# A software-pipelined graph network kernel: the hand-written order of all four engines' steps is replaced by another order

## The reference

```python
h = max(layernorm(x), 0);  x = x + cheb(h, adj)      # 4 Chebyshev orders of L = I - D^-1/2 A D^-1/2
h = max(layernorm(x), 0);  x = x + att_net(h, adj)   # h1 = tanh(h We + be), two attention layers, 3-layer MLP
#   v, q, k = tanh(h @ w + b);  att = softmax((q k^T) * mask - 9e15 * (1 - mask));  h' = att @ v
#   z = relu([h2, h3] W1 + b1);  z = relu(z W2 + b2);  z W3 + b3
h = max(layernorm(x), 0);  x = x + relu(norm(adj + I) @ (h @ Wg))
h = max(layernorm(x), 0);  t = adj @ h;  x = x + where(t > 0.5, 1, 0 * t)
```

## Time and profile before

| | |
|---|---|
| median of 3 runs | 851.47 us (851.32 to 852.67) |
| the profiled execution's own time | 851.93 us |
| its span in the profile | 849.8 us |
| PE busy | 768.0 us, 90% |
| DVE, ACT, POOL busy | 66%, 52%, 43% |

### The profile page before, as it was taken

One profiled execution on the slowest core, in us unless ns is written; L12 is line 12 of the kernel. 1 busy time (PEld: TensorE's weight loads), 2 busy tenths in 40 slices (PEclk: granted clock), 3 DMA queues, 4 the chain that ended last, 5 costly groups with the idle time before them and its releaser, 6 DMA issues.

```text
span 849.8 us, 11643 instructions
## 1 busy us (share of the span) xinstructions
PE 768.0 (90%) x3846; PEld 538.0 (63%) x3880; DVE 560.4 (66%) x1631; ACT 445.5 (52%) x929; POOL 363.6 (43%) x492
## 2 busy tenths in 40 slices
PE   7787999989999998999999898999989899998865
PEld 4455666766766676766667576676767667665533
DVE  4656677676767767676776768676676867675432
ACT  3164727474563747466473746547374645726330
POOL 4343545253444526354453525345461634542200
PEclk9999999999999999999999999999999999999995
DMA  6000102020010202010020202002020200000000
GB/s 189 28 2 6 51 1 63 1 62 1 13 51 1 62 1 62 0 39 25 1 63 1 62 1 63 1 1 63 1 62 1 63 1 6 2 0 7 1 6 6
DMA packets 29323, 22.77 MB, mean 27 GB/s; under 512 B 19536, under 2 KB 21072, under 8 KB 29264
## 3 DMA queue, kind: packets, MB, share of 16 engines
q1 hardware_dynamic: 28272, 21.80, 8.9%
q10 hardware_dynamic: 992, 0.23, 0.1%
HBM read 19.93 MB, written 2.10 MB: 26 GB/s over the span
## 4 chain that ended last, share of the span: by engine, by line
PE 53%; POOL 15%; issue 15%; DVE 12%; ACT 5%; POOLq 0%; ACTq 0%; DVEq 0%
PE turn_ps L1155 13%; PE pre_ps L1021 8%; PE post_ps L1021 4%; PE pre_ps L1038 4%; POOL rstd_pre L448 3%; PE turn_ps L1138 3%; POOL k_lo L525 2%; PE pre_ps L980 2%; DVE h_nat_pre L760 2%; POOL centred_pre L451 2%; PE qkv_ps L1089 2%; DVE score_ps L853 2%; PE qkv_ps L1094 2%; PE post_ps L1170 2%; DVE h_nat_pre L752 2%
## 5 line engine op out<-in xcount | busy, mean ns | idle before, releaser
L639 ACT ACTIVATE negz<-negz,negmax 128x512 f32<-128x512 f32 x128 | 92.2, 721 | 64.3 <-DVE negmax L861 64.2
L448 POOL TENSOR_TENSOR rstd_post<-vareps_post,nhalf 128x4 f32<-128x4 f32 x32 | 32.8, 1024 | 203.1 <-DVE vareps_post L742 203.1
L1155 PE MATMUL turn_ps<-pt,v_n 128*128 128x512 f32 x256 | 115.2, 592 | 0.0
L853 DVE TENSOR_TENSOR score_ps<-score_ps,a_nat 128x512 f32<-128x512 f32 x128 | 89.1, 696 | 17.6 <-PE score_ps L1124 16.7
L861 DVE CUSTOM_DVE_ANT_0 negz<-score_ps,gate 128x512 f32<-128x512 f32 x128 | 88.6, 692 | 4.4
L598 ACT ACTIVATE y_t_pre<-pre_ps 128x512 f32<-128x512 f32 x48 | 28.7, 597 | 115.0 <-PE pre_ps L1021 115.0
L1021 PE MATMUL pre_ps<-at_hi,u_pair_pre 128*128 128x512 f32 x192 | 84.8, 441 | 2.9 <-DVE u_pair_pre L780 2.6
L646 ACT ACTIVATE pt<-turn_ps 128x512 f32<-128x512 f32 x128 | 74.0, 592 | 17.9 <-PE turn_ps L1138 15.8
L448 POOL TENSOR_TENSOR rstd_pre<-vareps_pre,nhalf 128x4 f32<-128x4 f32 x32 | 33.9, 1060 | 113.5 <-DVE vareps_pre L742 113.5
L1138 PEld LDWEIGHTS turn_ps<-ident,negz 128*128 128x128 f32 x512 | 60.7, 140 | 32.5 <-issue 15.9
L1138 PE MATMUL turn_ps<-ident,negz 128*128 128x128 f32 x512 | 75.4, 275 | 1.9 <-ACT negz L639 1.7
(11 more groups left out here) (157 smaller groups left out, 1764.0 us busy)
## 6 DMA issues: line engine op xcount, KB each, us to landing
a_nat<-in_adj SPq DMA_DIRECT2D x15, 1024.0 KB, 6.1
x_in<-in_x SPq DMA_DIRECT2D x16, 128.0 KB, 2.8
out<-x_out SPq DMA_DIRECT2D x16, 128.0 KB, 1.9
a_nat<-in_adj SPq DMA_DIRECT2D x4, 256.0 KB, 4.8
cheb_ws<-in_L_gnn_weight ACTq DMA_DIRECT2D x2, 64.0 KB, 3.3
att_w<-in_L_gnn_a_wv SPq DMA_DIRECT2D x2, 64.0 KB, 3.8
att_w<-in_L_gnn_a_wk SPq DMA_DIRECT2D x2, 64.0 KB, 3.6
att_w<-in_L_gnn_a_wq SPq DMA_DIRECT2D x2, 64.0 KB, 3.3
```

What stands on the lines that cost most here:

```text
L448: gp.tensor_tensor(rstd[t][:], vareps[t][:], nhalf[:, 0:RB], ALU.pow)\
L639: sc.activation(probs[:, i, :], negz[:, i, :], ACT.Exp, bias=negmax[:, i:i + 1], scale=-1.0, accum_out=total[:, i:i + 1]).then_inc(probs_d ...
L853: ve.tensor_tensor(score_ps[i % 2][:], score_ps[i % 2][:], a_nat[s][:, i, :], ALU.mult)\
L1155: mm = te.matmul(turn_ps[0][:], v_n[a][:, j * P:(j + 1) * P], pt[:, j, :], start=(j == 0), stop=(j == RB - 1))
```

## The change

Only the two tables are rewritten. Every step is still there once for each graph, and no step's code is touched.

```diff
 ORDER = {
     "tensor": """
-        queries.1-1 turn_a0-0 turn2.2-2 turn3.2-2 keys.1-1 turn_a1-0 spread_inv.2-2 values.1-1
-        turn_a2-0 turn_a3-0 attend.2-2 scores0.1-1 cheb_ht-0 scores1.1-1 scores2.1-1 mlp1-2
-        turn0.1-1 cheb_weights-0 scores3.1-1 turn1.1-1 mlp2-2 turn2.1-1 cheb_prop3-0 turn3.1-1
-        mlp3-2 cheb_fold3-0 spread_inv.1-1 attend.1-1 cheb_prop2-0 queries.2-1 cheb_fold2-0
-        gcn_prop-2 keys.2-1 gcn_fold-2 cheb_prop1-0 scores0.2-1 cheb_fold1-0 values.2-1 scores1.2-1
-        scores2.2-1 turn0.2-1 last_prop-2 enc_ht-0 scores3.2-1 turn1.2-1 encode-0 last_fold-2""".split(),
+        queries.1-1 turn_a0-0 turn3.2-2 turn_a1-0 keys.1-1 attend.2-2 turn_a2-0 turn_a3-0
+        scores0.1-1 spread_inv.2-2 scores1.1-1 cheb_ht-0 values.1-1 scores2.1-1 mlp1-2
+        cheb_weights-0 scores3.1-1 turn0.1-1 turn1.1-1 mlp2-2 cheb_prop3-0 turn2.1-1 turn3.1-1
+        mlp3-2 cheb_fold3-0 spread_inv.1-1 attend.1-1 cheb_prop2-0 queries.2-1 gcn_prop-2
+        cheb_fold2-0 keys.2-1 gcn_fold-2 cheb_prop1-0 scores0.2-1 cheb_fold1-0 scores1.2-1
+        values.2-1 scores2.2-1 turn0.2-1 last_prop-2 enc_ht-0 scores3.2-1 last_fold-2 encode-0
+        turn1.2-1 turn2.2-1""".split(),
     "scalar": """
-        exp3.2-2 queries.1-1 copy_pt2.2-2 copy_pt3.2-2 copy_at0-0 keys.1-1 row_sum0-0 copy_at1-0
-        row_sum1-0 values.1-1 copy_at2-0 row_sum2-0 copy_at3-0 copy_inv.2-2 row_sum3-0 cheb_ht-0
-        exp0.1-1 exp1.1-1 copy_pt0.1-1 mlp1-2 exp2.1-1 copy_pt1.1-1 mlp2-2 exp3.1-1 copy_pt2.1-1
-        cheb_copy3-0 copy_pt3.1-1 copy_inv.1-1 cheb_copy2-0 queries.2-1 gcn_copy-2 keys.2-1
-        cheb_copy1-0 values.2-1 exp0.2-1 exp1.2-1 copy_pt0.2-1 enc_ht-0 last_copy-2 exp2.2-1
-        encode-0 copy_pt1.2-1""".split(),
+        values.2-2 copy_pt0.2-2 encode-1 exp3.2-2 copy_pt1.2-2 queries.1-1 copy_pt2.2-2
+        copy_pt3.2-2 copy_at0-0 copy_at1-0 keys.1-1 copy_at2-0 copy_at3-0 copy_inv.2-2
+        row_sum0-0 row_sum1-0 row_sum2-0 cheb_ht-0 row_sum3-0 exp0.1-1 exp1.1-1 values.1-1
+        mlp1-2 exp2.1-1 copy_pt0.1-1 copy_pt1.1-1 exp3.1-1 mlp2-2 cheb_copy3-0 copy_pt2.1-1
+        copy_pt3.1-1 copy_inv.1-1 cheb_copy2-0 queries.2-1 gcn_copy-2 keys.2-1 cheb_copy1-0
+        exp0.2-1 exp1.2-1 last_copy-2 enc_ht-0 exp2.2-1""".split(),
     "vector": """
-        stats_cheb-0  invert.2-2  norm_cheb-0 split_at0-0 split_at1-0
-        split_at2-0 split_at3-0 attend.2-2 mask0.1-1 mask1.1-1 cheb_ht-0 mask2.1-1 
-        cheb_weights-0 mask3.1-1  invert.1-1  mlp3-2
-        cheb_fold3-0 stats_gcn-2 attend.1-1 norm_gcn-2 cheb_fold2-0 gcn_fold-2 stats_last-2
-        mask0.2-1 cheb_fold1-0 stats_enc-0 norm_last-2 mask1.2-1 norm_enc-0 mask2.2-1 enc_ht-0  mask3.2-1  last_fold-2""".split(),
+        stats_cheb-0 invert.2-2 split_at0-0 split_at1-0 norm_cheb-0 split_at2-0 split_at3-0
+        mask0.1-1 attend.2-2 mask1.1-1 cheb_ht-0 mask2.1-1 cheb_weights-0 mask3.1-1 invert.1-1
+        mlp3-2 stats_gcn-2 cheb_fold3-0 attend.1-1 norm_gcn-2 cheb_fold2-0 gcn_fold-2
+        stats_last-2 mask0.2-1 cheb_fold1-0 stats_enc-0 norm_last-2 mask1.2-1 norm_enc-0
+        mask2.2-1 enc_ht-0 mask3.2-1 last_fold-2""".split(),
     "gpsimd": """
-        norm_cheb-0 add_cheb_bias-0 split_qk.1-1 mask_bias-1 roots-0 cheb_u3-0 more_roots-0
-        norm_gcn-2 split_qk.2-1 cheb_f0-0 norm_last-2 norm_enc-0
-        add_mlp_bias-0""".split(),
+        norm_enc-1 norm_cheb-0 mask_bias-1 split_qk.1-1 add_cheb_bias-0 roots-0 cheb_u3-0
+        more_roots-0 norm_gcn-2 split_qk.2-1 cheb_f0-0 add_mlp_bias-1 norm_last-2""".split(),
 }
```

## The result

The changed kernel takes 818.88 us (818.30 to 820.25, 4 runs) against 852.07 before (4 runs): a ratio of 0.9615, 95% interval 0.9602 to 0.9628. The profiled execution took 818.34 us with a span of 816.2.

A forecast was written before the change was run, and what follows sets the result against it. PE was taken as the bound, with about 4.5 of each 49.00 us period waiting. 13 periods at 1.3 (16.9), plus 1.3 and 1.0, minus 0.9, made 18.3: 851.93 to 833.6, stated as 833.5 us, range 823 to 848.

The forecast's parts named there:

- c1's add: DVE's c add ahead of `cheb_prop1`, 1.52 beside POOL's q_lo before, was to run with q_lo already over.
- The walk: Following the new lists from `attend.1` at 450.36 to the next, with durations from the rows: period 47.45 instead of 49.00.
- ACT's part ahead of `queries.1`: `copy_pt0.2` behind `exp2.2` and `values.2` ends near 474.95, ACT's `encode` near 475.6; `queries.1` starts there, 0.2 worse.
- `norm_cheb` in DVE's chain: Between `queries.1` and `scores0.1`: needs the port between q_lo and k_lo, ends near 483.9, then DVE has no gap.
- The rounding up from 47.45 to 47.7: Period taken as 47.7, because every tie (k_lo, `copy_pt0.2`, `norm_cheb`, DVE's chain) can only go one way.
- One reading in the prediction: After `keys.1` in the old trace: `values.1` could start at 479.32, starts at 480.33, 1.0 lost where 0.84 is listed.
- the rounds outside the full ones: Round 2 up to `attend.1` gains 1.3, round 16 about 1.0, the drain loses 0.9.
- More than reckoned: Chance 0.12: the kept stalls at `last_prop` and `keys.1` shrink, period 47.0, 823.5 us.
- The slower rival: Chance 0.13: `mask_bias` ahead of `split_qk.1` on POOL lies fully on the path, its 1.90 added: period 49.6, 860 us.
- Lost ties: Chance 0.22: x3's add waits for POOL's k_lo, or `norm_cheb` for x_b, taking 0.45 to 0.9 a period: 838 to 846 us.
- The signs to look for: Profile after: period near 47.7, `values.1` and `scores2.1` waits gone, `last_prop` 0.8 to 1.1, small ones at `keys.1`, `cheb_weights`.
- The reason that I gave for `last_prop`'s wait: Chain keys.2, k_lo, f0, x1, statistics, `last_prop` is not shortened anywhere; the largest stall of the round stays, 0.25 later.

The follow-up runs named there:

- the first half: Kernel before with the new order only from `queries.1` to `attend.1`, on all engines: 821.61 us, ratio 0.9638, period 47.02.
- the second half: Kernel before with the new order only in the rest of the round and the handover between rounds: 851.60 us, ratio 0.9989, period 48.97.
- the run with the gate back: Changed kernel with POOL's `mask_bias` behind `split_qk.1` again: 819.64 us, ratio 0.9620, period 46.93.
- the last run: Changed kernel with `add_mlp_bias` behind `norm_enc`, plus `keys.2` ahead of `gcn_prop` on PE and of `gcn_copy` on ACT: 836.30 us, ratio 0.9816.
- the run with the row sums back: Changed kernel with ACT's row sums strung between the adjacency copies again, as before the change: 830.40 us, ratio 0.9753, period 47.52.

## Why the prediction was wrong

**The direction and the mechanism were right.** `attend.2` behind `keys.1`, with `values.1` after it, covers the taking of the keys, the adjacency copies and the splits; the first half carries the gain (1.98 of 2.07 in the run of its own), and the second half is even. `last_prop` was to come 19.29 after `attend.1` with its wait left over; it came 451.35 - 432.11 = 19.24 after. c1's add came off q_lo, as stated, and took 0.42. `keys.2`'s place: 9.42 forecast, 9.30 measured.

**The step that failed is the size of a period.** The walk gave 47.45, I wrote 47.7, and it is 46.93. Laid out from `attend.1`, forecast and measured:

| | walk | after |
|---|---|---|
| last_prop | 19.29 | 19.24 |
| queries.1 | 25.25 | 24.99 |
| keys.1 | 27.7 to 27.95 | 27.47 |
| attend.2 | 28.75 | 28.44 |
| scores0.1 | 33.10 | 32.77 |
| mask0.1 on DVE | 34.95 | 34.45 |
| split of h done | 39.20 | 38.54 |
| next attend.1 | 47.45 | 46.93 |

On PE the 0.77 are 0.26 up to `queries.1`, 0.07 from there to `scores0.1`, 0.19 from there to `attend.1`, and 0.25 of rounding up.

- *ACT's part ahead of `queries.1`* was reckoned too long: I let `exp2.2`, `values.2` and `copy_pt0.2` follow each other at 0.84, 0.59 and 0.59, where the starts after are 0.72, 0.48 and 0.47 apart. `keys.1` was to start 2.7 after `queries.1`; it is 2.48, as before.
- *`norm_cheb` in DVE's chain.* The walk had it end near 483.9, 33.5 after `attend.1`, and DVE then without a gap. It ended at 463.96, 31.85 after `attend.1`, right behind q_lo and not behind k_lo, and DVE then waited 1.39 for the adjacency copies, which come behind `attend.2` on PE (the two rows below). So the splits, `mask0.1` and the split of h came 0.5 to 0.65 earlier than walked (0.33 of it from PE's own earlier place), and `cheb_weights`, for which I had a wait of 0.4, has none.
- *The rounding up from 47.45 to 47.7*, with the sentence that every tie can only go one way. It went the wrong way: the walk had already put each producer late, and a late producer that PE doesn't wait for costs nothing. `scores0.1` with k_lo was such a tie and cost 0.07.

```profile
462.72 1.24 DVE L758 COPY h_nat_pre<-h_nat_pre 128x256 f32<-128x256 f32 x1
465.36 1.29 DVE L764 TENSOR_TENSOR at_lo<-pre_ps,at_hi 128x512 fp32r<-128x512 f32 x2 [1.39 <-ACT at_hi L568]
```

One reading in the prediction is wrong, though the sum doesn't rest on it alone: 1.0 lost ahead of `values.1` where the wait is listed with 0.84. The bias matmul that the trace lacks stands in that gap, so 0.8 was lost for a wait of about 0.6. That a wait costs more than is listed holds all the same: ahead of `last_prop` 1.0 was lost for the 0.81 listed (`turn0.2` started at 467.95 and takes 0.44).

13 x 0.77 = 10.0 us of the 15.3 between forecast (833.6) and measured (818.3, profiled executions) are this.

**The other 5.3 are the rounds outside the full ones.** The forecast had 1.4 for them, they gave 6.7. The start up to `attend.1` of round 1 was left out of the sum, and it gained 2.7; by how much this is firm is open, for it ends at 57.4 to 59.1 in the runs that leave its order nearly alone. From there to round 2, 1.3 was forecast and 1.1 came, behind a lower clock (0.96 against 1.00) that hides some of the gain. Round 16 was given 1.0 and gained 2.6. The drain was charged 0.9, and the stretch from `attend.1` of round 16 to the end is 0.3 shorter.

**The rivals.** "More than reckoned" had 0.12, and its period (47.0) is nearly the measured one, its 823.5 us nearer than the forecast's. Of the two stalls that it named, `keys.1`'s stayed as before the change, but `last_prop`'s grew, so it was right in the size more than in the reason. The slower rival, `mask_bias` on the path, is refuted by the run that moves it back: no difference. Lost ties: x3's add took 0.42 after. `norm_cheb`'s copy was blocked, for 1.24, as before, but with no effect on the period, as the run with the gate back shows.

**The signs to look for.** No waits of `values.1` and `scores2.1`: right. A wait of 0.8 to 1.1 at `last_prop`: right, 1.07. Small new ones at `keys.1` and `cheb_weights`: none is listed; at `keys.1` 0.2 go to ACT's taking of the queries. The reason that I gave for `last_prop`'s wait (keys.2, k_lo, f0) was half of it: in the changed kernel POOL's end (centring done at 450.05) and DVE's own list (450.08) tie, and the last run shows that the list alone holds it.

## What to carry to other kernels

With in-order queues, look for the longest step that needs nothing recent (here 3.4 us of `attend.2`) and put it directly behind the step whose result goes round the other engines (`keys.1`). But the lists of those engines must be laid for it as well: the same move alone was 1.6% slower, half of it because PE's clock fell behind the longer wait; the whole new order with the move taken back was 0.4% slower; and both together were 3.9% faster. When such an order is walked, take start-to-start times and not lengths, sum every round (the partial ones gave a fifth of the gain), and don't add a margin on top of waits that are already pessimistic.

## What the runs showed of the hardware that I had not expected

That DVE and POOL shut each other out of a port was in the rows before. What I hadn't expected is that it reaches the smallest instructions. DVE's add on 4 elements a partition (L740) took 0.40 instead of 0.17 while POOL centred 256: it ended at 450.08, POOL's centring at 450.05. `norm_cheb`'s first instruction took 0.93 before the change, where it ended behind POOL's x_b, 0.47 after, and 1.42 in the run with the row sums back, where it ended behind k_lo. The Trainium skill (SBUF — State Buffer, Who interferes with whom) has issue order decide who is blocked; these rows fit that, though no run here isolates the pair.

The other is what one wait more can cost on PE. In the run with `attend.2` alone moved, five waits of 1.68 us were each followed by a fall of the granted clock to 0.50, and each fall cost 1.66 us, as much again as the wait; eight waits of the same length were followed by none. The changed kernel, whose longest wait in a full period is 1.07, has a clock of 1.00 in all of them.
